# Spectral bins half a step higher with matrices in eight chunks, and attention in four column tiles with sums from GpSimd

## What is computed

```python
def _L0_ffn_ref(x, sigma, phi, M_u, M_phi_plus, M_phi_minus, log_weights, gumbel):
    def _stu_conv(phi, u, n):                       # n = 8192, K = 16 filters
        sgn = jnp.where(jnp.arange(sl) % 2 == 0, 1.0, -1.0)
        Vf = jnp.fft.rfft(phi, n=n, axis=0)
        Uf_p = jnp.fft.rfft(u, n=n, axis=1)
        Uf_m = jnp.fft.rfft(u * sgn3, n=n, axis=1)
        U_plus = jnp.fft.irfft(Vf[None, :, :, None] * Uf_p[:, :, None, :], n=n, axis=1)[:, :sl]
        ...
    out = einsum('btkd,k,kde->bte', U_plus, sigma ** 0.25, Mpp) + (the same of U_minus and Mpm)
    for i, frac in enumerate((1, 2, 4, 8)):
        xi = x[:, :T // frac]
        si = _stu(xi, ..., M_u[i], M_phi_plus[i], M_phi_minus[i])   # with three taps M_u[i] in time
    ...
    return jnp.sum(stacked * weights, axis=-1)      # weights: hard choice with a soft part

def _L2_conv_ref(x, w_qkv, w_out, b_out):           # 4 heads of 32
    q, k = l2norm_axis1(q), l2norm_axis1(k)
    sim = jnp.einsum('bihd,bjhd->bhij', q, k) * 10.0
    attn = jax.nn.softmax(sim, axis=-1)
    out = jnp.einsum('bhij,bjhd->bhid', attn, v)
    ...
    out = jnp.einsum('bxyd,dc->bxyc', out, w_out) + b_out
```

## Time and profile before

| | before |
|---|---|
| median of 3 runs | 9300.02 us |
| the runs | 9278.6, 9300.02, 17873.6 us |
| profiled execution | 9263.69 us |
| its span | 9261.9 us |
| mean granted clock | 0.896 |
| PE busy | 7254.6 us (78%) |
| DVE busy | 6461.8 us (70%) |
| ACT busy | 4717.5 us (51%) |
| POOL busy | 4250.9 us (46%) |

### The profile page before, as it was taken

How to read it: one execution, slowest core, us unless ns; L and a number is a source line. 1 busy time by engine, 2 the same in 40 slices (tenths; PEclk the granted TensorE clock), 3 DMA queues, 4 the chain that set the end, 5 groups by cost and what they waited for, 6 DMA issues and landing times. The chain is left out here.

```text
span 9261.9 us, 165385 instructions
## 1 busy us (share of the span) xinstructions
PE 7254.6 (78%) x63005; PEld 4679.2 (51%) x63005; DVE 6461.8 (70%) x8039; ACT 4717.5 (51%) x8987; POOL 4250.9 (46%) x3064
## 2 busy tenths in 40 slices
PE   5777778777777778774789999568479999996576
PEld 3444434443444444443778887357345555553354
DVE  7999899997999899994156565232366666553447
ACT  4666566665666466663156565223224444454335
POOL 4999589994999599993300000000100000010005
PEclk8999999999999999996699999789769999998678
DMA  4555355553555355553432324631310000103010
GB/s 146 164 166 164 95 172 164 166 164 100 165 166 164 91 177 164 165 162 109 162 90 60 87 73 103 143 98 39 138 36 16 22 16 22 32 1 147 14 34 21
DMA packets 471266, 976.50 MB, mean 105 GB/s; under 512 B 128184, under 2 KB 226943, under 8 KB 453375
## 3 DMA queue, kind: packets, MB, share of 16 engines
q1 hardware_dynamic: 469490, 938.16, 34.1%
q10 hardware_dynamic: 960, 27.53, 1.1%
HBM read 822.11 MB, written 114.81 MB: 101 GB/s over the span
## 5 line engine op out<-in xcount | busy, mean ns | idle before, releaser
L892 POOL TENSOR_TENSOR ss_work<-ss_dtu,ss_ringb 128x768 f32<-128x768 f32 x1536 | 2761.5, 1824 | 259.1 <-POOLq L59 255.6
L754 PE MATMUL ss_ps<-ss_work,ss_ident 128*128 128x512 f32 (+1 forms) x6144 | 2309.6, 522 | 628.8 <-POOL ss_work L902 601.1
L754 PEld LDWEIGHTS ss_ps<-ss_work,ss_ident 128*128 128x128 f32 x6144 | 1198.2, 203 | 1521.0 <-issue 1319.3
L876 DVE TENSOR_TENSOR_SCAN ss_work<-ss_ps,ss_last,ss_work 128x768 f32<-128x768 f32 x1024 | 1811.3, 1804 | 67.6 <-ACT ss_ps L807 56.8
L807 ACT ACTIVATE ss_ps<-ss_dt,ss_a_neg 128x768 f32<-128x768 f32 x1536 | 1374.6, 895 | 289.0 <-DVE ss_work L876 272.0
L861 DVE TENSOR_TENSOR ss_work<-ss_work,ss_ps 128x1152 f32<-128x1152 f32 x768 | 1021.6, 1330 | 1.2 <-ACT ss_ps L815 1.2
L2658 DVE TENSOR_REDUCE at_top<-at_ps 128x1 f32<-128x384 f32 x1512 | 728.4, 547 | 400.1 <-PE at_ps L2576 399.9
L2639 ACT ACTIVATE at_probs<-at_ps 128x768 f32<-128x768 f32 x864 | 653.7, 808 | 657.7 <-PE at_ps L2595 656.8
L876 DVE TENSOR_TENSOR_SCAN ss_work<-ss_ps,ss_work 128x768 f32<-128x768 f32 x512 | 878.9, 1745 | 50.6 <-issue 17.5
L1409 DVE COPY mb_mix<-mb_ps 128x432 f32<-128x432 f32 x1088 | 633.7, 631 | 390.1 <-PE mb_ps L1432 389.9
L1499 ACT ACTIVATE mb_mix<-mb_ps 128x432 f32<-128x432 f32 x1088 | 613.0, 619 | 444.9 <-PE mb_ps L1432 439.0
(11 more groups left out here) (558 smaller groups left out, 9743.2 us busy)
## 6 DMA issues: line engine op xcount, KB each, us to landing
ss_ringb<-scan_rows SPq DMA_DIRECT2D x768, 384.0 KB, 3.6
ss_ringc<-scan_rows SPq DMA_DIRECT2D x768, 384.0 KB, 3.9
c_w<-in_l_ffn_w SPq DMA_DIRECT2D x52, 1024.0 KB, 12.6
mb_mats<-fq_mats ACTq DMA_DIRECT2D x8, 3360.0 KB, 16.5
at_packs<-at_high SPq DMA_DIRECT2D x64, 288.0 KB, 5.5
fq_mats<-fq_mats_high SPq DMA_DIRECT2D x8, 2048.0 KB, 9.2
fq_bins<-tb_out SPq DMA_DIRECT2D x68, 216.0 KB, 1.9
mb_bins_by<-fq_bins SPq DMA_DIRECT2D x34, 432.0 KB, 3.7
```

What stands on the lines that cost most here:

```text
L754: return pe.matmul(acc[:, d * WIN + a:d * WIN + e], ident[:, :], weighed[:, t % DEEP, d, a:e], start=n == 0 and e - a == 512, stop=n == NS ...
L876: dve.tensor_tensor_scan(hid[:, t % DEEP, d, ::step], decay[d][:, ::step], drive[:, t % DEEP, d, ::step], start, ALU.mult, ALU.add).then_i ...
L892: pool.tensor_tensor(drive[:, t % DEEP, d, :], dtu[:, t // NST % 2, d, :], ringb[:, t % RING, :], ALU.mult).then_inc(s["driven"], 1)
```

## The change

**Bins.** The frequencies lie half a step higher, at (2f + 1)/2 steps. There is no bin at zero or at the middle any more, so segments have 48, 24, 12 and 9 slots, and these divide by three: 31 trios. The two halves of the slots are now parts of 16 and 15 trios. The turned rows take all 128 partitions instead of 100. `from_bins` loads 96 and 90 rows, each in one DMA.

**Before the bins.** A new stage `taps_to_bins` holds the branch weights, all loads in one queue with x behind `fe`, the taps, and the first set of matrices, which DVE and ACT make in five pieces. Taps are taken from PSUM in one pass by ACT, and DVE reads PSUM again for the rest. The norm follows, then `to_bins` with the four phases; sets 1 to 3 of the matrices are made there by DVE and ACT between their copies, and POOL has no work in the spectral unit before mixing.

**Mixing.** The matrices are loaded in eight chunks of 105x2048. At the start the first is on ACT and seven on SP; at a change ACT asks for each once the last trio's fills of that part are made.

**Attention.** `v` has no ones. `apply` is four column tiles, one for each head and half of the queries, 32 rows by 192 columns. POOL adds the `probs` of two blocks into `added`; `sum_up` multiplies this with `ones_v`, in four tiles beside the values. `keep` waits for the sums too. DVE inverts 128x192 at once, POOL multiplies in four products of 32x192 in period 2 of a chunk; DVE does that for the last chunk.

```diff
-SEG_SLOTS = (49, 25, 13, 9)
+SEG_SLOTS = (48, 24, 12, 9)
 TRIO = 3
-SEG_TRIOS = tuple(-(-n // TRIO) for n in SEG_SLOTS)
...
 SLOTS_F = TRIO * TRIOS
-HALF_SLOTS = SLOTS_F // 2
+PART_TRIOS = ((TRIOS + 1) // 2, TRIOS // 2)
+PART_SLOTS = tuple(TRIO * n for n in PART_TRIOS)
...
+        taps_to_bins(nc, w, x_dram, ps, U, turned, fe, fa, sign, far, far_r, mats, lags, wgt, root, taps_dram)
+        norm_and_turn(nc, "fq_ln", U[:, :, :, :], U[:, :, :, :], 1e-5)
+        to_bins(nc, w, ps, U, turned, fe, fa, mats, lags, wgt, bins_dram, mats_dram)
+    mix_bins(nc, w, bins_dram, taps_dram, mats_dram, prod_dram, back_dram)
...
+                    sp.dma_start(dst, src).then_inc(s["few_loaded"], 16)
+                sp.dma_start(sign[:, :], w["sign"]).then_inc(s["few_loaded"], 16)
+                sp.dma_start(fe[:, :, :], w["fe"]).then_inc(s["fe_loaded"], 16)
+                for b in range(B):
+                    rows = x_dram[b * S:(b + 1) * S, :].rearrange("(a r) c -> a r c", r=RES)
+                    sp.dma_start(flat[ROWS_T * (b % 2):ROWS_T * (b % 2) + ROWS_T, RES * (b // 2):RES * (b // 2) + RES, :], rows).then_inc(s["x_loaded"], 16)
+                sp.dma_start(far[:, :], w["far"]).then_inc(s["far_loaded"], 16)
+                for dst, src in ((mats[0][:, :], w["mats"][0]), (lags[0][:, :], w["lags"][0])):
...
+                    act.activation(split[:, n % RING_T, :], bank(GROUPS_K + n)[0:STACK, 0:COLS], ACT.Copy, scale=root[:, :]).then_inc(s["rounded"], 1)
...
+                for n in range(TRIOS):
+                    dve.wait_ge(s["rounded"], n + 1)
+                    low = split[TAPS:2 * TAPS, n % RING_T, :]
+                    dve.scalar_tensor_tensor(low, bank(GROUPS_K + n)[TAPS:2 * TAPS, 0:COLS], root[TAPS:2 * TAPS, :], low, ALU.mult, ALU.subtract).then_inc(s["lowered"], 1)
...
+                for q in range(PIECES):
+                    raw, total_m = pieces[q][0], pieces[q][1]
+                    dve.tensor_scalar(total_m, raw, wgt[0:raw.shape[0], 0:1], None, ALU.mult).then_inc(s["summed"], 1)
+                for q in range(PIECES):
+                    dve.wait_ge(s["cut"], q + 1)
+                    dve.tensor_tensor(pieces[q][3], pieces[q][1], pieces[q][2], ALU.subtract).then_inc(s["cut_low"], 1)
+                dve.wait_ge(s["cut_low"], PIECES)
...
+                def gather(ph, q):
+                    if q == 0:
+                        dve.wait_ge(s["raw_loaded"], 32 * (ph + 1))
+                        if ph:
+                            dve.wait_ge(s["cut_low"], PIECES * ph)
+                    raw, total = pieces[q][0], pieces[q][1]
+                    dve.scalar_tensor_tensor(total, raw, wgt[0:raw.shape[0], ph + 1:ph + 2], total, ALU.mult, ALU.add).then_inc(s["summed"], 1)
+
+                def lower(ph, q):
+                    dve.wait_ge(s["cut"], PIECES * ph + q + 1)
+                    dve.tensor_tensor(pieces[q][3], pieces[q][1], pieces[q][2], ALU.subtract).then_inc(s["cut_low"], 1)
+
+                for ph in range(PHASES):
...
+        def load_mats(eng, n, chunk):
+            part = slice(chunk * PIECE, (chunk + 1) * PIECE)
+            eng.dma_start(mats[:, part].bitcast(F32), mats_dram[n, :, part]).then_inc(chunk_loaded[chunk], 16)
 
...
-                def load_mats(n, h):
-                    part = slice(h * HALF_E * P, (h + 1) * HALF_E * P)
-                    act.dma_start(mats[:, part].bitcast(F32), mats_dram[n, :, part]).then_inc(s[f"mats_loaded{h}"], 16)
...
                                 keep_back(act, copy, s["back_act"], c - 2, stretch // 2)
-                            if c in LAST and h == 1 and stretch == 0:
-                                load_mats(LAST[c] + 1, 0)
-                    if c in LAST:
-                        act.wait_ge(s["made"], filled(c, 1, FILLS - 1) + 1)
-                        load_mats(LAST[c] + 1, 1)
...
                 load_taps(0)
-                load_bins(0)
+                for chunk in range(1, 2 * CHUNKS_H):
+                    load_mats(sp, 0, chunk)
+                    if chunk == CHUNKS_H - 1:
...
-                                rows = back_dram[first:first + STEP, SLOTS_F * half + lo:SLOTS_F * half + hi, :].rearrange("i p x -> p i x")
-                                sp.dma_start(Z[lo:hi, n % RING_Z, half, u, :, :], rows).then_inc(s[loaded[n % RING_Z]], 16)
+                            rows = back_dram[first:first + STEP, PART_ROWS[0] * half:PART_ROWS[0] * half + PART_ROWS[half], :].rearrange("i p x -> p i x")
+                            sp.dma_start(Z[0:PART_ROWS[half], n % RING_Z, half, u, :, :], rows).then_inc(s[loaded[n % RING_Z]], 16)
...
                     at_least(pe, s["kept"], c)
-                for h in range(2):
-                    ins = pe.matmul(acc[64 * h:64 * h + 64, 0:R], v[:, j, 2 * pair + h, :, :].rearrange("p a d -> p (a d)"), probs[:, n % 4, h, :],
+                for tile, h, part in tiles():
+                    ins = pe.matmul(acc[DH * tile:DH * (tile + 1), 0, :], v[:, j, 2 * pair + h, :], probs[:, n % 4, h, part],
...
+            def sum_up(p):
+                j = p % PAIRS_J
+                pe.wait_ge(s["added"], p + 1)
+                for tile, h, part in tiles():
+                    ins = pe.matmul(acc[DH * tile:DH * (tile + 1), 1, :], ones_v[:, :], added[:, p % 2, h, part],
+                                    start=False, stop=j == PAIRS_J - 1, skip_group_check=True)
+                ins.then_inc(s["summed"], 1)
...
                     for g in due[3:]:
                         maxima(g)
+                    if p:
+                        sum_up(p - 1)
                     apply(2 * p)
                     apply(2 * p + 1)
                     if build is not None and p == BLOCKS // 2 - 3:
                         turn()
+                sum_up(BLOCKS // 2 - 1)
 
         @block.scalar
...
 
             def keep(c):
                 act.wait_ge(s["used"], (c + 1) * NT_)
+                act.wait_ge(s["summed"], (c + 1) * PAIRS_J)
                 at_least(act, s["divided"], c)
-                act.activation(kept[:, :], acc[:, 0:R], ACT.Copy).then_inc(s["kept"], 1)
+                act.activation(kept[:, :, :], acc, ACT.Copy).then_inc(s["kept"], 1)
 
...
 
-            def half_inverted(c, half):
-                dve.wait_ge(s["sums_ready"], c + 1)
-                part = inv[:, half * R // 2:(half + 1) * R // 2]
-                dve.reciprocal(part, part).then_inc(s["inverted"], 1)
+            def invert(c):
+                dve.wait_ge(s["kept"], c + 1)
+                at_least(dve, s["divided"], c)
...
+            def add(p):
+                pool.wait_ge(s["weighed"], 2 * p + 2)
+                at_least(pool, s["summed"], p - 1)
+                pool.tensor_tensor(added[:, p % 2, :, :], probs[:, 2 * p % 4, :, :], probs[:, (2 * p + 1) % 4, :, :], ALU.add).then_inc(s["added"], 1)
...
-                        ins = pool.tensor_tensor(*rows_of(c, h), ALU.mult)
-                    ins.then_inc(s["divided"], 1)
+                for p in range(BLOCKS // 2):
+                    add(p)
+                    if p >= PAIRS_J and p % PAIRS_J == 2:
+                        c = p // PAIRS_J - 1
+                        pool.wait_ge(s["inverted"], c + 1)
+                        pool.wait_ge(s["added"], p + 1)
+                        divide_in_turn(pool, c)
 
```

469 lines of the change are left out of this document (241 added, 228 removed).

## The result

The changed kernel took 9041.27 us (median of 4 runs, 8990.72 to 9065.97), the kernel before 9289.31 in the same comparison; the ratio is 0.9738, with an interval of 0.969 to 0.9785. So the change is 2.6% faster, 248 us by the medians. One of the four runs of the kernel before took 17873.6 us, which nothing on record explains; the ratio leaves it out, and without it the medians differ by 237 us. The forecast was 9020, in a range of 8950 to 9120. The profiled execution has a span of 9038.1 us, 223.8 less than the one of before; the forecast's sum was 261 less.

What follows compares the result with a forecast made beforehand. Mixing and attention were taken as bound by TensorE, from_bins by DMA. Terms −102, −28, −6, −12, −11, −6 and −96 (attention) sum to −261; from 9263.7 that gives 9003, with 17 added 9020 us; range 8950 to 9120.

Steps and rivals of the forecast that it cites:

- The forecast case: Whole kernel: 9020 us, 8950 to 9080 by its own terms, chance .60.
- Three trios fewer: Mixing: 31 trios for 34, at 34.1 us each, −102 us.
- Chunks at the changes: Mixing's three changes of matrix: loads in eight chunks, issued earlier, win back −28 us (−10 to −39).
- Start of mixing: First fill of mixing: an eighth of the matrix is enough for it, −6 us (0 to −12).
- To_bins: Sorting into bins: 62 trios for 68 at the mean of two clocks, −12 us.
- The rival on the clock: Bins: clock high throughout, −38 us, whole 8980 (.10); low throughout, +37, whole 9057 (.05).
- Before the first turn: Stretch before to_bins: x loaded beside the taps, norm last, first turn earlier by −11 us (0 to −25).
- From_bins: From_bins, bound by DMA: reads 186 rows for 204, 1.3 MB less, −6 us.
- Tiles: Attention's v phase: six groups of four column tiles, 0.16 us each, save 0.32 us in 432 periods, −138 us.
- Keep: Attention, chunk ends: keep waits for the sums and PE for keep, 0.76 us at each end, +30 us.
- The last pair: Attention's last pair of heads, without maxima: POOL's additions and products bind there, +7 us against the gain booked.
- The other side: Attention: POOL's additions block DVE's reductions, period 4.0 us, +310 us, whole 9330, up to 9450; chance .03.

Runs made afterwards that it cites:

- the last kernel above: The changed kernel with sums early, products on DVE in the last pair only, far and first matrices behind eight tap stores: 9010.46 us, ratio 0.9709.

## Why the prediction was right, and where its terms were off

The forecast case came true, with 21 us less gained than its number: by the medians 9041 for 9020. The terms promised more than that: 261 us, where the profiled executions differ by 223.8. A part of it was the profile that they started from, 26 us under the median of 9289 of its kernel, for which the forecast had added 17; from that median the sum gives 9028, 13 us below the measured one.

- **Three trios fewer** (−102): measured 3 × 33.75 = −101. Right.
- **Chunks at the changes** (−28): −22 between the two profiles, −27 between the means of all. The bound that the rows of the hole set was right: DMA is full there, and what is left is the loads' price, as the run without them shows (14 to 27 us).
- **Start of mixing** (−6): 12.5 us sooner, of which the first trio gives 4.7 back (36.8 us for 32.1) while the other chunks arrive: −8.
- **To_bins** (−12): +2.5 between the two profiles. The step that failed is the two clocks' mean: I took the profile's two and two phases as the rule, and it was the luckiest of three executions of that code (297.6, 314.3, 333.3 us). Against the mean of the three, 315, the new code's usual 300 to 305 is a gain of about 12; that this is just my term is luck, for three executions are few for a mean. The rival on the clock was right in direction. The same may be why the undisturbed runs of before stand above its profiled one: of the eleven runs of that kernel beside the last kernel above, the shortest, 9248.02 us, has a mean granted clock of 0.898 and the longest, 9305.89, one of 0.890. In which stage they differ is not shown.
- **Before the first turn** (−11): −9.7, but not by the working given. I had no pause of the taps in it. The loads of x beside the taps make ACT wait 23.3 us for a store, and so most of the time that the parallel load saved is spent there. Two runs with other orders took 1 us more and 4 less, so the bytes set most of this.
- **From_bins** (−6): −8.7.
- **Tiles** (−138): the period fell by 0.33 us (3.37 to 3.04, in the last pair 2.34 to 2.01), × 432 = −143. The price of 0.16 us for a group of four tiles, worked out from tiles of 512 columns at half the clock, held to the hundredth. The Trainium skill's price for matmuls that aren't decoded in hardware (TensorE: Matmul & The Clock Gate, "Wait — 56ns, not 53.3ns?") does not apply: four records in 0.163 us are 41 ns each.
- **Keep** (+30): the wait for keep is 0.75 us, as I had it, but the period of an end is 0.93 us longer than its neighbours (3.97 for 3.04), in the last pair 0.94 (2.96 for 2.02): +37.
- **The last pair** (+7): from its first exponential to its last it took 124.8 us for 126.3, a gain of 1.5 of the 17.8 that 54 periods would give; I had 11 us of loss, keep's 4 with them, and it was 16, of which 5 are keep's. POOL's four products are 2.6 us as I had them, but they are one piece, and ACT's next exponentials wait for the addition behind them: a period of 3.75 in a run of 2.01, though additions and products are only 19.1 us of a chunk's 21.1. I had taken POOL's sum over a chunk, and the pause comes from its longest piece.
- **Not booked: the pairs' starts.** This is the term that failed. I took the 0.32 us off every one of the 432 periods, but in the seven pairs with maxima the first seven periods end with a wait for the packed operands, whose loads do not get faster: in the fourth pair 23.6 us became 24.5, where 21.3 would have been the forecast's. Over the seven pairs 155.6 us became 159.6, where 0.33 off each period would have given 139.4. That is 20 us, against the 5 that I had guessed for starts. The row of before had the wait in it (17.8 us, released by DMA); I had not read it.
- **Not booked, and small: the reciprocal.** One of 1.34 us a chunk in a period with about 0.6 us to spare costs 0.35 to 0.47 us; before there were two of 1.34 in periods with 0.9 to spare, and one cost 0.15. That is some 3 us over the seven pairs, by the periods' lengths. The other way, the stretches between the pairs became 7 us shorter and what lies outside the pairs 3, which I had at nothing. In sum −143 + 37 + 12 + 20 + 3 − 7 − 3 = −81, where −74 was measured; 7 us are not accounted for.
- **The other side**: that additions hold up reductions is refuted by 548 ns with one addition a period and with two; DVE's products of two SBUF operands are held to an addition's end (1.89 us for 0.35). Both agree with the Trainium skill (SBUF — State Buffer, "Who interferes with whom"), by which the shared port is an exclusive lock that a reduction does not take. The rival's threshold, DVE held over 0.8 us a period, was seen in another way: with 1.5 us of products on DVE more a chunk, the pairs with maxima lost 123 us (112 in all, for the last pair gained 10).

## What to carry to other kernels

Ask of each engine's new work not only how much it is a period, but how long its longest piece is, and whether what stands behind that piece is waited for: four products in a row cost more here than POOL's sum would say. Before a saving is multiplied by a count, take out the periods that end with a wait for something the saving does not move, such as a load. Another order of the loads may gain little where the bytes of the stretch fill the DMA engines: here it was 4 us at best, of a pause of 23. And a stage whose clock differs between executions needs more than one profile before a term of a few per cent of it is booked.

## What the runs showed of the hardware that I had not expected

- A pause of PE of 1.87 us was followed by 4.5 us at a granted clock of 0.62, so that the same group of matmuls took 1.45 us for 0.83. Of 35 such pauses 32 were followed by a lower clock, three were not.
- Four matmuls on four column tiles start within 0.02 us of each other, and the next four 0.163 us later (192 columns of f32 at 2.4 GHz).
- What work on DVE beside POOL's additions costs depends on its operands: a DVE product of 0.35 us took 1.89 beside an addition, a reciprocal and a reduction their usual 1.34 and 0.55.
- PE stopped for 2.3 us in the middle of a group, with no semaphore to wait for, while the DMA share was 1.03, and went on 2.6 us behind the start of a late packet of queue 8. Without the loads two pauses over 1 us were left, for seven.
- Phases of the same bins matmuls ran at 2.4 GHz in two, one or none of four phases of the same code: 297.6, 314.3 and 333.3 us for the stage.
